# Four PSUM banks instead of three for the transposed scores, and the projections moved into the bank of the attention's output

## What is computed

```
h      = layernorm(xn) * ln1_g + ln1_b
q,k,v  = h WQ + bQ, h WK + bK, h WV + bV            16 heads of 8 features
attn   = softmax(q k^T / sqrt(8)), causal, window of 128 tokens
states = scan(s = A s + h Bw)                       over the tokens
g      = sigmoid(h Wg + bg)
x1     = xn + g (attn v WO + bO) + (1 - g) (states Cw)
s      = x1 + gelu(layernorm2(x1) W1 + b1) W2 + b2

f      = rms-normalised bf16(xn)
ffn    = bf16(xn) + sum over the 2 best of 8 experts (weight * expert(f))
out    = x + s * silu(ffn)
```

## Time and profile before

| | |
|---|---|
| median of 3 runs | 1056.16 us (1053.68 to 1056.58) |
| the profiled execution | 1053.38 us, span 1051.6 us, mean granted TensorE clock 0.932 |
| TensorE matmul busy | 901.4 us, 86% of the span |
| VectorE, ScalarE, GpSimd busy | 69%, 71%, 48% |
| chain that ended last | TensorE 50%, VectorE 21%, issue 14%, ScalarE 10% |

### The profile page before, as it was taken

How to read it: one execution, slowest core, us unless ns; L and a number is a source line. 1 busy time by engine, 2 the same in 40 slices (tenths; PEclk the granted TensorE clock), 3 DMA queues, 4 the chain that set the end, 5 groups by cost and what they waited for, 6 DMA issues and landing times.

```text
span 1051.6 us, 38097 instructions
## 1 busy us (share of the span) xinstructions
PE 901.4 (86%) x15768; PEld 554.8 (53%) x15768; DVE 726.6 (69%) x1747; ACT 742.0 (71%) x1302; POOL 500.0 (48%) x786
## 2 busy tenths in 40 slices
PE   2486999989889898989999998989989898988896
PEld 1243564645556464555556464555646455554535
DVE  8255687777768677777768677876858687766415
ACT  3224787867868786777878787776868677766755
POOL 6323547272644627364554727363553736433331
PEclk7556999999999999999999999999999899999969
DMA  5743513434160333425151333425142242510000
GB/s 103 141 99 63 112 31 107 53 106 65 48 124 19 111 53 102 66 77 96 47 115 29 109 55 103 65 78 94 48 103 31 93 66 67 96 37 7 26 2 11
DMA packets 85598, 75.15 MB, mean 71 GB/s; under 512 B 9458, under 2 KB 79155, under 8 KB 85427
## 3 DMA queue, kind: packets, MB, share of 16 engines
q1 hardware_dynamic: 83346, 71.93, 31.6%
q10 hardware_dynamic: 2080, 0.79, 0.3%
HBM read 36.26 MB, written 30.15 MB: 63 GB/s over the span
## 4 chain that ended last, share of the span: by engine, by line
PE 50%; DVE 21%; issue 14%; ACT 10%; DMA 2%; POOL 1%; SPq 1%; DVEq 0%; POOLq 0%; ACTq 0%
PE ps L567 7%; PE ps L507 6%; PE ps L705 5%; PE ps L765 5%; PE ps L726 5%; PE ps L496 4%; ACT pt L862 3%; DVE mx L1111 3%; DVE gc L1162 3%; DVE lin L1155 2%; PE ps L584 2%; PE ps L699 2%; PE ps L579 2%; PE ps L597 2%; PE ps L522 2%
## 5 line engine op out<-in xcount | busy, mean ns | idle before, releaser
L1111 DVE TENSOR_REDUCE mx<-ps 128x2 f32<-128x320 f32 (+1 forms) x512 | 226.4, 467 | 140.9 <-PE ps L522 136.2
L862 ACT ACTIVATE pt<-ps 128x1024 f32<-128x1024 f32 (+1 forms) x256 | 234.6, 916 | 124.8 <-PE ps L496 124.0
L1284 POOL TENSOR_SCALAR_AFFINE_SELECT pt<-pt 128x512 f32<-128x512 f32 x256 | 164.2, 643 | 228.0 <-ACT pt L862 227.6
L507 PE MATMUL ps<-kd,qz 48*32 48x160 bf16 (+1 forms) x4096 | 154.9, 240 | 68.1 <-DVE mx L1111 38.7
L496 PE MATMUL ps<-qz,kd 51*32 51x256 bf16 (+1 forms) x4096 | 176.3, 273 | 4.8 <-ACT pt L862 2.8
L507 PEld LDWEIGHTS ps<-kd,qz 48*32 48x32 bf16 x4096 | 77.9, 92 | 187.1 <-ACT pt L862 95.5
L567 PE MATMUL ps<-pt,va 128*32 128x256 f32 (+1 forms) x2048 | 157.9, 389 | 5.1 <-issue 4.5
L705 PEld LDWEIGHTS ps<-m,act_t 128*128 128x128 f32 x1024 | 126.8, 191 | 51.4 <-DVE act_t L1183 36.4
L705 PE MATMUL ps<-m,act_t 128*128 128x128 f32 x1024 | 143.2, 283 | 8.5 <-DVE act_t L1183 8.0
L1287 POOL TENSOR_SCALAR_AFFINE_SELECT pt<-pt 128x512 f32<-128x512 f32 x192 | 129.3, 674 | 0.0
L920 ACT ACTIVATE lin<-ps,mbias 128x512 f32<-128x512 f32 x128 | 87.6, 684 | 47.5 <-DVE act_t L1183 29.6
(11 more groups left out here) (172 smaller groups left out, 1630.4 us busy)
## 6 DMA issues: line engine op xcount, KB each, us to landing
qz<-qk_parts SPq DMA_DIRECT2D x32, 384.0 KB, 7.4
kd<-qk_parts SPq DMA_DIRECT2D x32, 384.0 KB, 9.2
qk_parts<-qp SPq DMA_DIRECT2D x16, 384.0 KB, 2.6
qk_parts<-kp SPq DMA_DIRECT2D x16, 384.0 KB, 2.4
xl<-L_attn_x SPq DMA_DIRECT2D x16, 256.0 KB, 3.5
qk_parts<-qp SPq DMA_DIRECT2D x16, 256.0 KB, 3.0
qk_parts<-kp SPq DMA_DIRECT2D x16, 256.0 KB, 2.7
xnr<-xn SPq DMA_DIRECT2D x16, 256.0 KB, 3.2
```

The costliest lines, as they stand in the source:

```text
L507: nc.tensor.matmul(ps[QG * c:QG * (c + 1), 4 + par, w * pr:w * (pr + 1)], qz[q][rows, 2 * g + pr, P * i + QG * c:P * i + QG * (c + 1)], kd ...
L862: nc.scalar.activation(to, src, ACT.Exp, scale=SCALE).then_inc(exp_ok.sem, 1)
L1111: nc.vector.tensor_reduce(mx[:, i, HG * g + pr:HG * (g + 1):2], src, AX.X, ALU.max).then_inc(mx_ok.sem, 1)
L1284: sel1 = nc.gpsimd.affine_select(out=pt[:, s, :, 0:P], in_=pt[:, s, :, 0:P], compare_op=ALU.is_ge, fill=0.0, base=0, pattern=[[0, HG], [1, ...
```

## The change

The transposed scores get four banks: 0 and 1 for even steps, 2 and 3 for odd ones. Half 1's wait for the exponential of the step before is dropped. All that went through bank 3 goes through bank 7. That bank's other users lie in between, so the order of owners in a body is: state product, h, q, k, u, v, then the transposed attention output of the first half, then g, the combine matrix, the second half's output, ao, and the experts' sum. The waits follow that order. In ScalarE's stream the copy to `ot` stands before the exponential of step 10 instead of behind it. The waits of the second expert's `up` for readers of bank 3 are dropped.

```
 def pair(n):
-    return 2 * (n % 2), 1
+    k = 2 * (n % 2)
+    return k, k + 1

 def place(n, c):
     k = pair(n)
-    return 2 * sorted(k).index(k[1 - c % 2]) + c // 2
+    return 2 * k.index(k[1 - c % 2]) + c // 2

 scores():
-                if main and half == 1 and n >= 1:
-                    pe.wait_ge(*done(exp_ok, b, n))

 turn_out(b, g):
                 if g == 0:
-                    pe.wait_ge(*done(cb_ok, b - 1))
+                    pe.wait_ge(*(done(v_ok, b + 2) if has(b + 2) else done(s1_ok, b)))
+                elif has(b + 1):
+                    pe.wait_ge(*done(cT_ok, b + 1))
                 else:
                     pe.wait_ge(*done(ao_ok, b, g))

 turn_h0, project_q, _k, _u, _v, _g, states, turn_combine and their readers:
-    bank(3)
+    bank(7)

 project_g():
                     pe.wait_ge(*done(v_ok, b + 2))
+                    pe.wait_ge(*done(ao_ok, b, 1))

 states():
                     pe.wait_ge(*done(st_ok, b))
+                    pe.wait_ge(*done(cb_ok, b - 1))

 turn_combine():
-                    pe.wait_ge(*(done(gth_ok, b + 2) if nx2 else done(s1_ok, b)))
+                    pe.wait_ge(*(done(gth_ok, b + 2) if nx2 else done(ao_ok, b, 1)))

 up(e), e == 1:
-                        pe.wait_ge(*done(s1_ok, b))
-                        if nx2:
-                            pe.wait_ge(*done(gth_ok, b + 2))
                         if nxt:
-                            pe.wait_ge(*done(cT_ok, b + 1))
                             pe.wait_ge(*done(nmT_ok, b + 1))

 ScalarE's loop, at n in (10, 18):
+                    the copy to ot (same lines), now ahead of the exponential of step n
                     if main and n < NCH:  the exponential
-                    the copy to ot
```

More of the change, by code:

```diff
@@ L615, in project_v @@
                     for t in range(NT):
-                        mm = nc.tensor.matmul(bank_t(3)[:, t], hT[:, P * t:P * (t + 1)], wv[:], start=False, stop=True, skip_group_check=True)
+                        mm = nc.tensor.matmul(bank_t(7)[:, t], hT[:, P * t:P * (t + 1)], wv[:], start=False, stop=True, skip_group_check=True)
                     mm.then_inc(v_ps.sem, 1)
@@ L810, in v_in @@
                     nc.scalar.activation(va[:, (b + 2) % 3].rearrange("p t g k v -> p t (g k) v")[:, :, :, 0:DH],
-                                         bank_t(3).rearrange("p t (h v) -> p t h v", v=DH), ACT.Copy).then_inc(v_ok.sem, 1)
+                                         bank_t(7).rearrange("p t (h v) -> p t h v", v=DH), ACT.Copy).then_inc(v_ok.sem, 1)
                 def gate_in():
@@ L815, in gate_in @@
                     act.wait_ge(*done(x1_ok, b - 1))
-                    nc.scalar.activation(gth[:, (b + 2) % 3], bank_t(3), ACT.Tanh, scale=0.5).then_inc(gth_ok.sem, 1)
+                    nc.scalar.activation(gth[:, (b + 2) % 3], bank_t(7), ACT.Tanh, scale=0.5).then_inc(gth_ok.sem, 1)
                 def square(t):
@@ L836, in hT_in @@
                     act.wait_ge(*done(g_ps, b + 1))
-                    nc.scalar.activation(hT[:], bank(3), ACT.Identity, bias=cols["ln1_b"][:], scale=cols["ln1_g"][:]).then_inc(hT_ok.sem, 1)
+                    nc.scalar.activation(hT[:], bank(7), ACT.Identity, bias=cols["ln1_b"][:], scale=cols["ln1_g"][:]).then_inc(hT_ok.sem, 1)
                 def qk_in(n):
@@ L843, in qk_in @@
                     act.wait_ge(*done(signal_ps, b + 2))
-                    nc.scalar.activation(dst[:, 0], bank(3), ACT.Identity, bias=cols[bias][:]).then_inc(qkhi_ok.sem, 1)
+                    nc.scalar.activation(dst[:, 0], bank(7), ACT.Identity, bias=cols[bias][:]).then_inc(qkhi_ok.sem, 1)
                 if start(b, -2):
@@ L851, in body @@
                 for n in range(NCH + 4):
+                    if main and n in (NCH // 2 + 2, NCH + 2):
+                        g = int(n > NCH)
+                        act.wait_ge(*done(pv_ps, b, NCH // 2 * (g + 1)))
+                        act.wait_ge(*done(ott_ps, b, g))
+                        nc.scalar.activation(ot[:], bank(6), ACT.Copy).then_inc(ot_ok.sem, 1)
                     if main and n < NCH:
@@ L889, in body @@
                         act.wait_ge(*done(down_ps, b - 1))
-                        nc.scalar.activation(cT[:, 1 - q], bank_bf(3), ACT.Copy).then_inc(cT_ok.sem, 1)
+                        nc.scalar.activation(cT[:, 1 - q], bank_bf(7), ACT.Copy).then_inc(cT_ok.sem, 1)
                     if nxt and n == 1:
@@ L1079, in qk_rest @@
                     dve.wait_ge(*done(qklo_ok, b + 1, n + 1))
-                    nc.vector.scalar_tensor_tensor(out=rest[:], in0=bank(3), scalar=cols[bias][:], in1=hi[:, 0],
+                    nc.vector.scalar_tensor_tensor(out=rest[:], in0=bank(7), scalar=cols[bias][:], in1=hi[:, 0],
                                                    op0=ALU.add, op1=ALU.subtract).then_inc(qkr_ok.sem, 1)
@@ L1086, in recur @@
                     dve.wait_ge(*done(ncw_ps, b - 1))
[L1087 removed]
+                    nc.vector.tensor_tensor_scan(st[0:N, (b + 2) % 3], acol[0:N, :].to_broadcast([N, T]), bank(7)[0:N], 0.0, ALU.mult, ALU.add).then_inc(st_ok.sem, 1)
                 def states_in():
@@ L1091, in states_in @@
                     dve.wait_ge(*done(xn_copied, b))
-                    nc.vector.tensor_tensor(s1[:], bank_t(3), xnr[:], ALU.add).then_inc(s1_ok.sem, 1)
+                    nc.vector.tensor_tensor(s1[:], bank_t(7), xnr[:], ALU.add).then_inc(s1_ok.sem, 1)
                 if start(b, -2):
```

23 lines of the change are left out of this document (9 added, 14 removed).

## The result

| | before | after |
|---|---|---|
| median, same chip | 1054.92 us (1051.86 to 1056.58, 4 runs) | 1029.91 us (1026.43 to 1031.52, 4 runs) |
| ratio | | 0.9762 [0.9725, 0.9799] |
| profiled span | 1051.6 us | 1029.8 us |
| mean granted clock | 0.932 | 0.991 |

What follows compares the result with a forecast made beforehand. TensorE's stream in the attention loop was taken as the bound. Terms 14.4 + 1.5 - 2.4 - 2.2 - 1.2 + 5.2 = +15.3 us on 1053.4, plus half of 2.8, gave 1070 us; range 1058 to 1080.

Steps and rivals of the forecast that it cites:

- What bounds the kernel: Attention loop: one TensorE stream carries three batches, so whatever holds it up moves the whole body; TensorE busy 86%.
- The removed wait: Half 1's wait for the exponential in the scores: worth at most 14.5 us, of which 2.4 and 2.2 credited.
- step 3: Attention loop: its 0.23 us wait gives nothing back, since half 1 of step 4 waits for VectorE's maximum anyway.
- Last batch: No plain scores there: 2.8 us of exponential waits go, some becoming waits for GpSimd's masks; -2.2 us.
- The wait of project_g for ao: G projection at step 12 stands still about 1.04 us in 14 batches, reaching the body's end; +14.4 us.
- turn_out and ot: ot ahead of exponential 10 delays va, so turn_out starts 0.3 us later in five of 14 batches; +1.5 us.
- step 10: Attention loop: its 0.18 us wait gives nothing back, since the v projection behind it needs VectorE's scan st.
- Stops in the middle of a run: Five unexplained TensorE stops after step 12; a pause ahead may shorten them, 0 to -2.5 us, taken as -1.2.
- The clock: The g projection's pause lowers the granted clock in 4.5 of 14 batches, 1.16 us each; +5.2 us.
- rival B: The g projection's pauses are too short to lower the clock; 1065 us, chance 0.22.
- D: Freed half 1 runs alongside half 0 at each step and pays back more than the pause costs; 1044 us, chance 0.07.
- signs of being wrong: Batch body gets shorter; mx waits shrink by over 10 us; or L608 waits appear while bodies are no longer.

Runs made afterwards that it cites:

- run 6: Kernel before, with only half 1's two waits put on separate instructions, half 0 keeping its double wait; 1028.25 us, ratio 0.9797.
- 7: Changed kernel, with half 0's two waits in the scores put on separate instructions; 1028.86 us, ratio 0.9786.
- Run 2: Changed kernel, with half 1's old wait for the exponential of the step before put back at every step; 1066.07 us, ratio 1.0132.
- run 3: Changed kernel, with an always-met wait (exponential of two steps before) at half 1's old place; 1052.8 us, ratio 1.0007.
- run 9: Changed kernel, with half 1's old wait put back only in the last batch; 1039.67 us, ratio 0.9889.
- run 1: Kernel before, with only the g projection's new wait for the first ao added; 1060.87 us, ratio 1.0105.
- run 4: Changed kernel, with the g projection one step later, at step 13 instead of 12; 1021.01 us, ratio 0.9714.
- run 5: Kernel before, three banks kept, with the double waits of both halves in the scores split onto separate instructions; 1025.85 us, ratio 0.9758.
- run 10: Kernel before with both halves' double waits split, plus 30 met double waits a batch among the experts' down matmuls; 1025.08 us, ratio 0.9772.
- run 8: Changed kernel, with half 1's old wait put back, but split onto the first transposed score matmul; 1051.96 us, ratio 0.9994.

## Why the prediction was wrong

**What bounds the kernel.** Right in the main: TensorE's stream sets the body, and half 1 of each step with its maximum is the link (6 against 7). But the list of waits was taken as the whole price of waiting.

**The removed wait: the step that failed.** The prediction let the wait be worth "at most 11.7 + 2.8 = 14.5 us" and credited 4.6. Run 2 puts it at 36 us, run 3 at 22.9 us for the mere instruction (26 by the ratios). It asked only how long the wait waited. Not asked was what the wait did to the instruction that it shared with the maximum's: two semaphores make a wait instruction of its own, 0.147 instead of 0.055 us after each maximum that half 1 waits for, and with these instructions amid the scores come most of the stops.

The argument for step 3, "half 1 of step 4 starts at 461.04 whatever step 3 did", took 0.14 to 0.15 us as a property of the chip. It was a property of that instruction, and what all "starts whatever" arguments rested on. Counted from the batch's first exponential, half 1 of step 4 starts after 6.11 us before (batch 6) and after 5.92 us in the changed kernel (batch 7).

**Last batch.** Sized at -2.2 us, measured -7.0; run 9 gives 7.2 for the wait alone. The waits of 2.8 us are in the earlier trace rows, but the stretch at clock 0.78 was not looked at: shorter pauses leave TensorE more of it at the upper level.

**The wait of project_g for ao.** Right: 14.4 forecast, 14 waits with 13.8 us measured, in full at the body's end (runs 1 and 4). In batch 7 of after:

```profile
527.97 0.49 DVE L1147 TENSOR_TENSOR ao<-ps,rz 128x128 f32<-128x128 f32 x2
528.60 0.38 PE L609 MATMUL ps<-bias,onesb 65*128 65x512 bf16 x1 [0.98 <-DVE ao L1147]
529.91 0.60 ACT L815 ACTIVATE gth<-ps 128x512 f32<-128x512 f32 x1 [1.79 <-PE ps L625]
```

528.60 - 528.46 = 0.14 us: here two waits stand before one matmul again, v's and ao's, and the change itself brought them in.

**turn_out and ot.** +1.5 us forecast. In batch 7 `turn_out` starts at 525.86, 0.15 us after va's end (525.08 + 0.63, in the row below), where it was 0.02; the list of waits has no row of L580 for va, so over the run it is a small loss, which no run here took apart.

```profile
525.08 0.63 ACT L809 ACTIVATE va<-ps 128x512 f32<-128x512 f32 x1
```

The v projection now waits for st in each batch (6.8 us, 16 times), which the prediction had named as what is late next at step 10.

**Stops in the middle of a run.** Forecast -1.2 of at most -2.5, as a side effect of the pause; measured -8.0, mostly an effect of the double waits (3, 5, 10). The prediction had looked only at those behind step 12, 2.5 of 12.7 us, and took the pause for what would shorten them; in run 1, with the pause alone, 11.3 us are left. The Trainium skill (Runtime: NRT & Kernel Launch, "Instruction fetch mechanics") has crossings between blocks mostly hidden. The trace agrees with the "mostly": 20 of the 122 instruction packets after the first exponential of before are followed by a stop, of up to 2.0 us, and one such packet in run 5 is.

**The clock.** +5.2 forecast, 0 measured at the pause. None of the 98 pauses ahead of the g projection (0.90 to 0.98 us, seven kernels) was followed by a fall, as rival B had it. The falls in bodies 1 to 13 stand behind the two pauses at the start of a loop or behind stops of 1.7 to 2.1 us, with one exception: in run 6 a single stop of 1.0 us was followed by one (the idle time before it, 0.42 us, had ended 4.4 us earlier). So a single idle stretch of that length can do it, and that none of the 98 did is not explained. The exception, with the clock of the stretches 874 to 877 and 877 to 880.4 us in run 6 (columns as in the earlier trace rows):

```profile
875.02 0.29 PE L496 MATMUL ps<-qz,kd 51*32 51x256 bf16 x3 [1.00 <-issue]
874.00:877.00 3.00, 1.86 (x73) 1.00 0.03 5
877.00:880.40 3.40, 3.40 (x72) 0.50 0.17 35
```

Here the pair at the start of batch 7's loop, after which the clock stayed up:

```profile
507.09 0.25 PE L508 MATMUL ps<-kd,qz 48*32 48x160 bf16 x4 [0.52 <-DVE mx L1110]
508.00 0.25 PE L508 MATMUL ps<-kd,qz 48*32 48x160 bf16 x4 [0.49 <-DVE mx L1110]
```

The Trainium skill's rule that short idle moments swing the clock (TensorE: Matmul & The Clock Gate, "A second HAM failure mode: psum-queue depth-cycling") fits the loop starts and not the pause of the g projection.

**The rivals.** D had the sign and nearly the size (1044 us, chance 0.07), with another mechanism: that halves of a step run at the same time. They already did where nothing waited; step 12 fills 0.56 us before and 0.57 after. Its 10 us for that were not there; the 0.09 us of each hand-over and the stops were. That it had the sign is therefore luck. The chances were wrong as well: 0.85 on slower rested on a gain capped by the list of waits. One of the prediction's own signs of being wrong came: the mean of bodies 0 to 13 went from 60.0 to 59.1 us.

**The sum, as measured**, in us of span: start +0.8; pause and hand-overs +7.5 in the undisturbed bodies (the pause is 16.5 of it, 1.18 x 14 by run 4, so the rest gave back 9.0; run 3 gives 0.67 x 14 = 9.4 to the instruction, all of it); disturbances -20.5; body 14 -2.5; last batch -7.0; together -21.7.

**Open.** Why TensorE's next instructions come too late more often where wait instructions stand amid the scores; the last 8 us of the disturbances in the sum; what adds 0.27 us at step 14 in run 8.

## What to carry to other kernels

Give each TensorE instruction one semaphore to wait for: put each wait on the first instruction that really needs it, even if the two stand side by side, and look for double waits first on the short hand-over that sets each step. Before a wait is priced by its row in the list, look at what else stands before the same instruction; a wait that is always met can cost 2% of a kernel. A step that inherits a bank belongs behind the point where the bank comes free, here one step later.

## What the runs showed of the hardware

- From the end of a VectorE maximum to the TensorE matmul that waits for it: 0.055 us with one semaphore, 0.147 with two, in every kernel of the study that has such hand-overs (medians, waits of more than 0.15 us).
- A wait instruction added at each half 1, always met, cost 22.9 us of 1030 amid matmuls of 0.24 us (run 3), and 30 such a batch amid the experts' matmuls cost nothing (run 10: 1025.08 against 1025.85 us).
- Stops in which no semaphore is waited for end 2.1 to 3.0 us after a 16 KB packet starts on the instruction queue (106 of 109 stops).
- None of 98 pauses of 0.90 to 0.98 us ahead of the g projection was followed by a fall of the granted clock; a single stop of 1.0 us in run 6 was. Two pauses of about 0.5 us within 1.1 us were followed by one in 2 to 5 of the 13 loop starts of bodies 1 to 13, for about 1.1 us each.
- Where the records of the clock begin late, the mean and the strip show full clock: after's strip has only nines at its start, yet its matmuls of 324 ns there are as long as before's.
